# Graph attention and experts on one core: runs of four tiles instead of two in the edge sums, with the score work moved behind the fourth tile

## The reference, cut to what matters

```python
# N = 6250 nodes, 256 features; src, dst: 206250 edges, sorted by dst
def gat_layer(x, W, b, a, g, beta):          # layer 1: 8 heads of 64; layer 2: one of 256
    h = x @ W.T + b
    score = (h @ a[:d])[src] + (h @ a[d:])[dst]
    e = exp(-leaky_relu(score, 0.2))
    out = segment_sum(e[:, None] * h[dst], src, num_segments=N)
    return layernorm(out) * g + beta         # then elu
x = x + elu(gat_layer(concat(elu(gat_layer(layernorm(x), ...)) for 8 heads), ...))
tokens = layernorm(x)                        # top 2 of 8 experts by a softmax router
out = x + tokens + sum_e combine[:, e] * (gelu(tokens @ w1[e] + b1[e]) @ w2[e] + b2[e])
```

## Time and profile before

| what | value |
|---|---|
| median of 3 runs | 6864.75 us (6851.06 to 6879.34) |
| profiled execution, its own time | 6873.33 us |
| its span in the profile | 6871.5 us |
| mean granted TensorE clock | 0.887 |
| PE busy | 5194.1 us (76%), 21312 products |
| DVE busy | 4274.9 us (62%) |
| ACT busy | 2400.3 us (35%) |
| POOL busy | 3275.6 us (48%) |
| HBM read | 816.28 MB |

### The profile page before, as it was taken

The page is one execution under the profiler, slowest core; times in us unless marked ns, Lnnn a source line. Parts: engine busy times, 40 slices in busy tenths (PEclk is TensorE's granted clock), DMA queues, the critical chain, the costliest instruction groups (busy, mean ns, idle before and its releaser), DMA issues. The chain is left out here.

```text
span 6871.5 us, 96747 instructions
## 1 busy us (share of the span) xinstructions
PE 5194.1 (76%) x21312; PEld 2884.9 (42%) x21312; DVE 4274.9 (62%) x15762; ACT 2400.3 (35%) x6496; POOL 3275.6 (48%) x3459
## 2 busy tenths in 40 slices
PE   4577888867777777777777775787777777787787
PEld 2322222233333333333333333565655655565565
DVE  4688999966667667766676763444444444444443
ACT  2005777722333333333333332233333333333333
POOL 0000000016666666666666664666666666666662
PEclk8789999988989999989999996888888888888888
DMA  2100000016666666766676675444444444444444
GB/s 82 46 1 0 0 0 0 0 34 197 201 196 202 196 199 198 206 198 199 200 202 197 198 190 132 114 114 115 118 114 117 113 115 112 116 114 112 116 115 54
DMA packets 325650, 847.59 MB, mean 123 GB/s; under 512 B 73909, under 2 KB 97661, under 8 KB 325256
## 3 DMA queue, kind: packets, MB, share of 16 engines
q0 software_dynamic: 224256, 690.38, 37.1%
q1 hardware_dynamic: 101000, 152.57, 7.5%
HBM read 816.28 MB, written 26.36 MB: 123 GB/s over the span
## 5 line engine op out<-in xcount | busy, mean ns | idle before, releaser
L988 POOL DMA_INDIRECT out_rows<-table,shared_node_of x1712 | 1634.4, 955 | 1007.2 <-issue 461.7
L988 POOL DMA_INDIRECT heads_rows<-table,shared_node_of x1712 | 1620.1, 946 | 1017.5 <-issue 461.8
L1174 PE MATMUL heads_banks<-heads_rows,heads_hot 128*128 128x512 f32 x3424 | 1844.9, 667 | 249.1 <-DVE heads_rows L1045 142.3
L1174 PE MATMUL out_banks<-out_rows,out_hot 128*128 128x256 f32 x3424 | 1272.9, 464 | 326.7 <-DVE out_hot L1049 173.8
L1045 DVE TENSOR_TENSOR heads_rows<-heads_rows,heads_ps_k 128x512 f32<-128x512 f32 x1712 | 1160.9, 678 | 1.0
L1121 ACT ACTIVATE sums<-heads_banks x856 | 510.1, 600 | 1790.0 <-PE heads_banks L1174 985.6
L1174 PEld LDWEIGHTS heads_banks<-heads_rows,heads_hot 128*128 128x128 f32 x3424 | 622.6, 205 | 792.3 <-issue 660.8
L1121 ACT ACTIVATE late_sums<-out_banks x856 | 326.0, 383 | 1780.7 <-PE out_banks L1174 1033.5
L1174 PEld LDWEIGHTS out_banks<-out_rows,out_hot 128*128 128x128 f32 x3424 | 671.9, 221 | 525.8 <-issue 382.1
L853 PE MATMUL sort_ps_a<-sort_by_tile,sort_by_lane 125*128 125x367 f16 x1650 | 542.1, 330 | 148.1 <-ACT sort_by_lane L766 83.6
L647 DVE TENSOR_SCALAR sort_by_tile<-sort_count_tiles_h,sort_src_i 125x367 f16<-125x367 f16 x1650 | 613.5, 379 | 0.3 <-issue 0.2
(11 more groups left out here) (345 smaller groups left out, 6690.1 us busy)
## 6 DMA issues: line engine op xcount, KB each, us to landing
heads_lanes<-lane_rows SPq DMA_DIRECT2D x214, 256.0 KB
out_lanes<-lane_rows SPq DMA_DIRECT2D x214, 256.0 KB
heads_rows<-table,shared_node_of POOLq DMA_INDIRECT x1712
out_rows<-table,shared_node_of POOLq DMA_INDIRECT x1712
table<-proj_rows SPq DMA_DIRECT2D x50, 253.9 KB
table<-mid_rows SPq DMA_DIRECT2D x50, 127.0 KB
proj_x_raw<-in_x POOLq DMA_DIRECT2D x5, 1250.0 KB, 15.7
moe_x_raw<-in_x SPq DMA_DIRECT2D x50, 125.0 KB
```

The costliest lines, as they stand in the source:

```text
L988: nc.gpsimd.indirect_dma_start(out=rows[:, g % RING, j, :], out_offset=None, in_=table[:, :], in_offset=bass.IndirectOffsetOnAxis(ap=node_ ...
L1174: ins = nc.tensor.matmul(banks[:, bass.ds(info[r], width)], hot[:, g % HOTS, j, :], rows[:, g % RING, j, 0:width], start=False, stop=True, ...
```

## The change

RUN becomes 4, so that a run is a group: PER = 1. The constants that follow from it: MOST_RUNS = (206250 + 4·128·50) // 512 = 452, MOST_TILES = STEPS = 1808, RUNS = GROUPS = 452, COLS = 1920. Per layer there are 24 more groups (96 more steps with their gathers), 452 clears instead of 856, 452 copies instead of 856. ACT's wait for PE's sum and PE's wait for ACT's copy each occur once a group, and PE may now be a whole group ahead of the copy that it waits for. `done_by` gives multiples of four.

In the group's order: on PE the scores of g+3 come behind tile 3 instead of tile 1; on ACT the weights of g+2 come behind the copy of the whole group; on DVE the adding up, the target score and the leaky maximum of g+2 come behind tile 3, in layer 1 with `make_hot` between.

```diff
-RUN = 2
+RUN = 4
@@ DVE, group g
-                if g + AHEAD < GROUPS:
-                    reduce_pieces(g + AHEAD)
                 if by_row:
                     dve.wait_ge(s["brought"], base["brought"] + g + 1)
                 weigh(g, 0)
-                if g + AHEAD < GROUPS:
-                    add_target(g + AHEAD)
                 extra.upto(g * GROUP)
                 weigh(g, 1)
-                if g + AHEAD < GROUPS:
-                    make_leaky(g + AHEAD)
                 extra.upto(g * GROUP + 1)
...
                 weigh(g, 3)
+                if g + AHEAD < GROUPS:
+                    reduce_pieces(g + AHEAD)
                 if by_row and g + AHEAD < GROUPS:
                     make_hot(g + AHEAD)
+                if g + AHEAD < GROUPS:
+                    add_target(g + AHEAD)
                 extra.upto(g * GROUP + 3)
+                if g + AHEAD < GROUPS:
+                    make_leaky(g + AHEAD)
@@ ACT
-                    if j == 1 and g + AHEAD < GROUPS:
+                    if j == GROUP - 1 and g + AHEAD < GROUPS:
                         make_weight(g + AHEAD)
@@ PE
-                    if j == 1 and ahead:
+                    if j == GROUP - 1 and ahead:
                         source_scores(g + SCORE_AHEAD, block_ids(info[2 * PER:]))
```

## The result

The changed kernel takes 7015.17 us (median of 4 runs, 7000.74 to 7019.57), the kernel before 6859.76 us beside it (4 runs): ratio 1.0218, 95% interval 1.0199 to 1.0237. It is slower by 155 us; 6600 us was forecast, and 7015 lies 45 us above the range.

The account below looks back on a forecast made before the run. The loop of PE, DVE and ACT was taken as the bound, with gathers early. From 6873.3 us, +112 + 63 - 88 - 165 - 230 + 46 - 4 = -266 gave 6607, predicted as 6600 us; range 6350 to 6970 us.

Parts of the forecast that it names:

- What bounds the kernel: Both edge sums: the loop of PE, DVE and ACT sets 6.11 us a group; gathers are early, POOL has time to spare.
- Part 1: Edge sums: 24 more groups a layer cost PE time alone, +112 us in heads and +63 us in out.
- Part 2: Edge sums on PE: 404 fewer clears a layer at 0.11 us, -88 us; fewer copies on ACT priced at nothing.
- Part 3: PE's waits ahead of clears and products: leads grow by two steps, stops shrink, -165 us in heads, -230 us in out.
- Part 4: The sort ahead of the edge sums: wider routes cost more, the one-partition chain over fewer runs less, together -4 us.
- The first: Weights of g+2 on DVE: the longer way back uses up the lead, no stop goes, slower at 7020 us; chance 0.16.
- The second: POOL's gathers in both edge sums become the bound once nearly all stops go, 6250 us; chance 0.14 with close cases.
- The clock: PE's clock, granted at 0.91 and 0.86: fewer stops might save 235 us in heads; left out, bends the range downward.

Follow-up runs that it names:

- third buffer: Changed kernel with three buffers of turned tiles (the transposed selection) on DVE instead of two: 7007.16 us, ratio 1.0193 to the kernel before.
- narrow products: Changed kernel with 64 columns in each edge product on PE instead of 512 and 256, the other sums left out: 7014.95 us.

## Why the prediction was wrong, step by step

**What bounds the kernel: half right, and it misled.** "So gathers are early" held on the first kind of chip: there gathered rows were waited for only 28 us in heads after the change. But POOL's row gave 4.9 us a group, only a fifth below 6.11, and I took that for time to spare. On chips of the second kind exactly this row, 4.98 us there against 5.01 in the body of the heads stretch, is the bound of both kernels. On either kind a group is paid whole.

**Part 1, the padding: failed.** "Their cost is PE time, if PE stays the engine that the others follow" gave +175 us, with +46 for the growth of the idle time that was to stay; the padding alone measured +331. PE was busy 76% of the stretch, and my own sentence said that no engine was full; a loop with an engine idle a quarter of its time charges a further turn with the idle time in it. The figure that I named and set aside, 24 x 6.11 x 2 = 293 us, was the nearer one.

**Part 2, clears: of the right size, not measured alone.** Priced at -88 us, with copies at nothing; with whatever stops they bring, runs of four measured -133.

**Part 3, the stops: the step that failed most.** "So both leads grow by two steps", 395 us less idle time. PE's idle time went from 1211 to 1217 us, 1.41 to 1.35 us a group. PE's waits ahead of clears and products, forecast at 400 and 350 us, are 566 in heads and 641 in out. Of the 415 us between 6600 and 7015, 355 are idle time that was to be 862 us and is 1217, and the rest is PE's busy time.

Two things in the step were wrong. One is a missed wait. PE's lead over the clears did grow, and their waits went. On DVE I listed what is queued behind the moved steps, and left out the turned tiles of g+4, which need the scores of g+2 and stand between DVE's third and fourth weighing; those scores had moved two steps later. So DVE's lead grew from two steps to three there, not to four, and the whole wait for the scores, 315 us in heads and 806 in out before, now stood at that line with 347 and 834.

The other is deeper, as the third buffer showed. It gave the fourth step of lead, and the wait went to the next users of PE's signals while the time stayed. Lead bought at one place didn't count here; and with PE's work cut by 662 us the group stayed too. That part was a model of single stops, each with a length that a lead can be subtracted from. The runs show a pace instead: 5.93 to 5.97 us a group in the changed kernel, its third buffer and its narrow products alike, and it goes away with the gathers. How gathers make PE's signals late there, and why the pace lands at just that value, I can't say; it was narrowed to the gathers, not explained.

**Part 4, the sort: right.** The first edge product came 3 us earlier (-4 forecast). PE's busy time was forecast at 2060 and 2040 us, and is 2120 and 2042; in heads a product lasted 680 ns in the mean instead of 667.

**The rivals.** The first had the time (7020) but not the cause: its place was the longer way back through ACT's copy and exponential. DVE never waited for the weights in heads (0.0 us ahead of their copy, L1080) and at most 6.5 us in out (L1049). The moves that make that way longer cost 75 us with runs of two, but gain some 51 with runs of four, and runs of four without any longer way back are already at 7066 us. What it had right is "nothing goes". The second, gathers as the bound, was to give 6250 us and a faster kernel; on the second kind of chip the changed kernel does take 6273 us for that very reason, but before takes 6008 there by the same bound.

**The clock.** I left it out of the sum. It follows the stops: in heads it was granted at 0.89 with PE idle 21% of the stretch after the change, 0.97 with 17% for the same kernel on the second kind of chip, 1.00 with 11% without gathers, where a product lasts 608 ns in the mean instead of 680, and 0.51, close to the lower level of 1.2 GHz throughout, with 46% in the narrow products. The Trainium skill, "TensorE: Matmul & The Clock Gate", section "What's actually happening", says that the slow level is the default and that activity lifts it; these four rows agree. The clock moved PE's busy time, not the length of a group: narrow products at half the clock gave the same 5.93 us.

## What to carry to other kernels

Where a change adds turns to a loop, charge each turn at the loop's measured period, not at the busy time of its busiest engine; only an experiment that pads and does nothing else tells the difference. Before trading instructions for padding, take the issuing queue's own rate (busy time plus unexplained idle time, per instruction) and ask whether the added turns go through it: a queue at 80% is the bound as soon as whatever hides it is gone. And a wait that follows a late signal from user to user (L1027, then L1013, then L1027 again) is no cause; before calling a wait new, look whether another line had it before. Stop moving it, and take away the suspected source altogether. Ask also what padding really does: here the last padding groups were dearer than real ones.

## What the runs showed of the hardware

- The same kernel takes 6860 to 6940 us on some chips and 6001 to 6008 us on others, 12 to 14% less, with repeats of a kernel on a chip within 0.6%. POOL's gather takes 0.95 us on both. What the traces show of the difference is TensorE's signals, late beside gathers: in heads ACT's copies had 811 us of idle time before them that no event of the profile ends on the first kind, 0 us on the second, and 0 us on the first kind too when the gathers were left out. The cause of the lateness is open.
- A gather of 128 rows costs POOL 1.245 us at its full pace (0.95 us busy, 0.30 us between), one of 64 rows 1.20 us. Rows of 520 and of 260 numbers cost nearly the same (0.949 and 0.959 us busy).
- At the end of each stretch, where the gathers name one row 128 times, the DMA share rises from 0.81 to 1.01 while 174 GB/s are moved instead of 242, and a group takes 6.8 us instead of 5.01 (second kind, heads).
- On the second kind of chip the change is worse, 4.4% against 2.2%: there POOL's price for a gather is the bound, and a shorter loop of PE, DVE and ACT gives nothing back for the added groups.
